# Four products without a reader after each step of TensorE while the first image is set up

## What is computed

```python
def block0(x):                       # attention, 8 heads of 16 channels, L = 1024 pixels
    hid = group_norm(x, 32 groups)
    q, k, v = qkv_w @ hid + qkv_b
    weight = softmax((q * scale).T @ (k * scale))     # 1024 x 1024 for each head and image
    a = weight @ v
    return x + proj_w @ a + proj_b

def block1(x):                       # 1x1 convolution and a feed-forward network of 512 features
    x = x + conv_w @ gelu(rmsnorm(x)) + conv_b
    return x + ffn_w2 @ gelu(ffn_w1 @ rmsnorm(x) + ffn_b1) + ffn_b2
```

## Time and profile before

| | |
|---|---|
| median of 3 runs | 1762.37 us (1761.8 to 1763.55) |
| time of the profiled execution | 1763.75 us |
| its span, first to last instruction | 1761.8 us |
| mean granted clock over the span | 0.975 |
| PE busy | 1698.3 us, 96% |
| DVE busy | 1492.8 us, 85% |
| ACT busy | 1366.5 us, 78% |
| POOL busy | 335.7 us, 19% |
| DMA | 106.18 MB, mean 60 GB/s |

### The profile page before, as it was taken

One profiled execution on the slowest core, in us unless ns is written; L12 is line 12 of the kernel. 1 busy time (PEld: TensorE's weight loads), 2 busy tenths in 40 slices (PEclk: granted clock), 3 DMA queues, 4 the chain that ended last, 5 costly groups with the idle time before them and its releaser, 6 DMA issues.

```text
span 1761.8 us, 33312 instructions
## 1 busy us (share of the span) xinstructions
PE 1698.3 (96%) x12402; PEld 693.2 (39%) x12402; DVE 1492.8 (85%) x2606; ACT 1366.5 (78%) x2480; POOL 335.7 (19%) x411
## 2 busy tenths in 40 slices
PE   3999999999999999999999999999999997699999
PEld 2333333333333333333333333333333332355555
DVE  4899999999999999999999999999999992455552
ACT  1288888888888888888888888888888887466664
POOL 4101111111111111111111111111111011322220
PEclk8599999999999999999999999999999999799999
DMA  5422323232323132324242324141313011233341
GB/s 111 64 44 52 61 41 71 46 66 43 70 40 73 40 72 38 76 37 75 36 76 37 76 36 76 33 67 35 67 35 66 10 21 38 79 104 110 107 109 72
DMA packets 61121, 106.18 MB, mean 60 GB/s; under 512 B 27296, under 2 KB 30112, under 8 KB 60960
## 3 DMA queue, kind: packets, MB, share of 16 engines
q1 hardware_dynamic: 58656, 95.66, 27.6%
q10 hardware_dynamic: 2304, 8.39, 1.2%
HBM read 34.48 MB, written 9.06 MB: 25 GB/s over the span
## 4 chain that ended last, share of the span: by engine, by line
PE 83%; DVE 11%; issue 2%; SPq 1%; DMA 1%; POOL 1%; ACT 1%; DVEq 0%; ACTq 0%; POOLq 0%
PE psum L607 26%; PE psum L578 25%; PE psum L591 10%; DVE maxes L865 9%; PE psum L673 6%; PE psum L561 4%; PE psum L645 2%; PE psum L647 2%; PE psum L646 2%; PE psum L549 2%; PE psum L514 2%; PE psum L690 1%; DVE stats L881 1%; DVE rows L849 1%; SPq L309 0%
## 5 line engine op out<-in xcount | busy, mean ns | idle before, releaser
L865 DVE TENSOR_REDUCE maxes<-psum 128x1 f32<-128x512 f32 x2048 | 1269.5, 680 | 92.3 <-PE psum L578 90.8
L779 ACT ACTIVATE probs<-psum 128x512 f32<-128x512 f32 x2048 | 1107.4, 600 | 219.2 <-PE psum L591 196.6
L578 PE MATMUL psum<-k_stack,q_stack 62*128 62x512 f32 x2048 | 785.6, 461 | 19.0 <-DVE maxes L865 8.9
L591 PE MATMUL psum<-q_stack,k_stack 64*128 64x512 f32 x2048 | 770.8, 455 | 1.2 <-ACT probs L779 1.1
L607 PE MATMUL psum<-probs,values 128*32 128x256 f32 (+1 forms) x6912 | 621.2, 431 | 0.5 <-ACT probs L779 0.5
L578 PEld LDWEIGHTS psum<-k_stack,q_stack 62*128 62x128 f32 x2048 | 329.5, 188 | 561.8 <-DVE maxes L865 445.7
L591 PEld LDWEIGHTS psum<-q_stack,k_stack 64*128 64x128 f32 x2048 | 318.7, 185 | 14.8 <-ACT probs L779 10.5
L607 PEld LDWEIGHTS psum<-probs,values 128*32 128x32 f32 x6912 | 136.2, 108 | 286.8 <-issue 228.7
L673 PE MATMUL psum<-probs,inv_den 128*128 128x512 f32 x256 | 116.5, 598 | 0.0
L411 POOL CAST parts<-neg_max 128x16 fp32r<-128x16 f32 x64 | 12.6, 196 | 538.2 <-DVE neg_max L841 538.2
L788 ACT ACTIVATE probs<-psum,params_sb 128x512 f32<-128x512 f32 x128 | 82.5, 685 | 20.6 <-PE psum L647 14.2
(11 more groups left out here) (82 smaller groups left out, 1044.6 us busy)
## 6 DMA issues: line engine op xcount, KB each, us to landing
q_stack<-q_high SPq DMA_DIRECT2D x256, 64.0 KB, 2.2
k_stack<-k_high SPq DMA_DIRECT2D x128, 128.0 KB, 4.0
x_sb<-in_x SPq DMA_DIRECT2D x16, 512.0 KB, 5.2
q_stack<-q_low SPq DMA_DIRECT2D x128, 64.0 KB, 4.0
k_stack<-k_low SPq DMA_DIRECT2D x64, 128.0 KB, 4.3
attn<-raw SPq DMA_DIRECT2D x128, 64.0 KB, 2.3
inv_den<-inv_den_rows SPq DMA_DIRECT2D x128, 64.0 KB, 2.3
values<-inv_rms_rows SPq DMA_DIRECT2D x16, 512.0 KB, 5.0
```

Of the source, the lines that this page charges most:

```text
L578: nc.tensor.matmul(psum[:, BANKS + tile % BANKS, :], q_stack[used, place, chunk // 4, p, 128 * (chunk % 4):128 * (chunk % 4) + 128], k_sta ...
L591: nc.tensor.matmul(psum[:, tile % BANKS, :], k_stack[used, place, p, 128 * chunk:128 * chunk + 128], q_stack[used, place, t, p, :], start= ...
L779: nc.scalar.activation(probs[:, tile % 8, :], psum[:, tile % BANKS, :], ACT.Exp, scale=SCALE).then_inc(probs_ready, 1)
L865: nc.vector.tensor_reduce(maxes[:, chunk // 4, j, 4 * p + chunk % 4, key_half:key_half + 1], psum[:, BANKS + max_tile(u, s, k) % BANKS, :] ...
```

## The change

In TensorE's stream a new function `keep_awake(n)` issues `n` products of the projection weights (`wp`, 128 by 128) with the matrix of the group means (`group_mean`, 128 by 128) into the first 128 columns of `acc`. They wait for nothing and signal nothing, and nobody reads what they write: the first real product into `acc` starts a new sum. Four of them follow each of the steps 10 to 15 of u = -2, and each step of u = -1 that is not broken.

That makes 6 x 4 = 24 products in u = -2. In u = -1, steps 0 to 2 have 12, all ahead of the first maximum tile, and steps 4, 5, 7, 8, 9, 11, 12, 14 and 15 have 36, each group of four between the last maximum tile of one step and the first of the next. 72 products are added in all, and nothing is taken away or moved.

```diff
+            def keep_awake(n):
+
+                for i in range(n):
+                    nc.tensor.matmul(acc[:, 0:C], wp[:, :], group_mean[:, :], start=True, stop=True)
+
             def slot(b, parity, half, part=None):
                 u = b * 2 + half
                 for s in steps_of(part):
...
                     weigh_before(u, parity, half, s, 0 if broken else QUARTER, HALF)
+                    if u == -1 and not broken or u == -2 and s >= 10:
+                        keep_awake(4)
```

## The result

The median went from 1762.32 us (4 runs, 1761.8 to 1763.55) to 1774.79 us (4 runs, 1772.72 to 1776.99). The ratio is 1.007, with a 95% interval of 1.0052 to 1.0087. The forecast was 1757.1, and the range ended at 1763.0. The profiled execution took 1776.99 us with a span of 1775.0, 13.2 more than the span before.

The account below looks back on a forecast made before the run. A chain paced by VectorE, with TensorE at half clock last at four broken steps, was taken as the bound. 5.8 + 0.3 + 2.25 - 1.2 - 1.9 = 5.25 us won, from 1762.37 to 1757.1; range 1754.2 to 1763.

Parts of the forecast that it names:

- What bounds the start: Up to unit 0: VectorE's reductions set the pace at about 0.605 us each, TensorE only at four broken steps.
- the check of the model: Broken steps at half clock: a modelled VectorE wait of 1.6 us, set against 1.44 to 1.82 in the trace.
- The gap: Before the first maximum tile: 0.2 us for the products and 1.7 for 3.4 us at half clock; tile 1.9 later.
- case B: The forecast: the clock falls in the gap and comes back in the fill; 1757.1 us, chance 0.44.
- The price per product: In the gap at full clock: 0.22 to 0.27 us per product, 8.5 us taken for the 36.
- The groups: Nine groups of four between maximum tiles: 0.13 us of VectorE waiting each at full clock, 1.2 us lost in all.
- The four breaks: Side jobs in the four broken steps: VectorE waits 0.4 us in place of 6.18 at full clock, 5.8 won.
- The first steps of unit 0: First tile of unit 0 to the group mean of step 3: 2.25 us won from the full clock.
- The ends of case B: Whole kernel: 1755.5 to 1759.5 us, given as following from the ends of the terms.
- Case C: Nine groups among the maxima at half clock cost 1.6 us each; slower, 1773 or 1785 us, chance 0.16.
- Case A: In the gap the clock never falls, so the 1.7 us are not lost; 1755.4 us, chance 0.28.
- The 5.3 us in the earlier trace: End of the attention: the clock came back after 5.3 us of dense products, called float32, in one place.

Follow-up runs that it names:

- e10: e9 plus one product at the end of each of the four broken steps; 1756.8 us, ratio 0.9967 to the kernel before.
- e1: The change with only its 36 products in the gap before the first maximum tile, without the nine groups between tiles; 1763.1 us, ratio 0.9999 to the kernel before.
- e5: The change with eight early products at steps 7 and 8 of u = -2, four fewer at step 2, and the nine groups moved to mid-step; 1760.8 us.
- e7: The change with eight early products at steps 7 and 8 of u = -2, four fewer at step 2 of u = -1, nine groups at step ends; 1772.7 us.
- e11: e7 with groups of four at the ends of all 13 steps from step 3 of u = -1, broken ones included; 1759.1 us, ratio 0.9984 to the kernel before.
- e9: e5 with each group of four split into three products behind the second tile and one behind the fourth; 1764.7 us, ratio 1.0009 to the kernel before.
- e3: The change with one product after each maximum tile, except at side jobs, in place of the nine groups; 1800.2 us, ratio 1.020 to the kernel before.
- e8: Early gap products as in e7, but using 64 rows instead of 128, and no groups between maximum tiles; 1762.5 us, one run.

## Why the prediction was wrong

**What bounds the start: right.** VectorE's rate between the breaks, its waits at half clock, and the way of the gain to the end all came out. (The fourth break waits 1.10 in the earlier trace rows, less than the 1.44 to 1.82 that the check of the model named.) In e10, where the clock is full, the group mean is at 79.85; the forecast for it was 80.8.

**The gap: the mechanism right, the size too small.** The clock fell and came back in the fill, as in case B, but it was down for about seven microseconds and not 3.4. The first tile came 3.2 late instead of 1.9. The price per product was right: at full clock e1 made the 36 in 8.28 us, where the sum had 8.5.

**The groups: this is the step that failed.** The sum put nine of them at 0.13 us each, 1.2 in all, on a clock that case B held full for the whole of the maxima. They cost 14.6, or 1.6 each, and 1.6 is what the prediction itself gave for a group at half clock. I took it that the mix of tiles and products as a whole would hold the clock, and did not look at the order in it. The order was in the code: a break in mid-step, then two tiles, then a whole step of tiles, and only then a group. e5 shows that the places count: the same nine groups in mid-step made the kernel 11.8 us faster than e7. e11 shows that more groups need not cost more: with four more, and behind the breaks, it was 13.5 us faster than e7. The price at full clock was a little low, 0.13 against 0.2 to 0.3 in e11; nine times that would be 1 us more and not 13. That the stretch of tiles alone is what makes the clock fall is an argument from these medians, and it is not shown: the falls in the traces of e7 and e11, and e9 against e5, do not fit it.

**The four breaks:** 6.18 to 0.4 was the sum; it was 3.8, with 0.20 at the one that ran wholly at full clock; in e10 the four wait 0.20, 0.29, 0.28 and nothing. **The first steps of unit 0:** 2.25 was the sum, 1.7 came, the clock being back at 96 only. **The ends of case B:** 1755.5 to 1759.5 are not what the ends of its terms add up to; by them it is 1753.8 to 1762.1, and 1774.8 is outside these too.

**The rivals.** Case C had the place, the mechanism and nearly the time: "if the clock falls once the maxima have begun", 1773. That the time came so near is in part luck: its sum had eight groups and 12.8 us where 14.6 came, 0.2 for the gap where the first tile came 3.2 late, and left out the 1.7 won in unit 0; these errors partly cancel. It had 0.16, and with a mechanism that the before trace showed for 39 us at a stretch, that was too little. The error was one of weight: the only rows on tiles with products among them were those around 83, where the clock rose, and those have both kinds of scores. For the order of the change there was no row at all, and the range should have held both ends of that: it stopped at 1763 where 1773 was worked out. Case A was seen in the gap of e1, and it is worth little by itself. The 5.3 us in the earlier trace rows were misread besides: the prediction calls them float32 products, but they are products of the type fp32r with all 128 rows, one record each (and not float32, as the text ahead of it says of all matmuls but the scores):

```profile
1521.69 0.77 PE L645 MATMUL psum<-q_stack,wconv_high 128*128 128x512 f32 x1 [1.08 <-ACT attn L757]
...
1526.94 0.47 PE L645 MATMUL psum<-q_stack,q_high 128*128 128x512 f32 x1
```

In the Trainium skill, "TensorE: Matmul & The Clock Gate", section "What's actually happening", the clock follows how busy the engine was. Busy time as the profile counts it does not show that here: from 68 to 76 TensorE is busy for 7.64 of 8 us at 0.50 in the changed kernel and for 7.49 at 1.00 in e10. (From 60 to 75 in the kernel before it was not quite without a break, as the prediction has it, but paused twice for 0.36 us. And the stacks of image 1 are wanted 19 steps of 2.8 us, some 53 us, behind the start of unit 0, and not 44. Nothing hangs on either.)

**What stays open.** Why the clock fell in some executions of e5, e9 and e11 and not in others, at 38.7 in e7, and at 53 in e3 without any change in the pattern, is not settled; no run moved only the moment at which a pattern begins. Nor is it settled what tells the tiles of maxima from the products: e8 speaks against the number of rows in the gap. The type fp32r alone is not it either, since the clock came back at 1527 behind 5.3 us of such products in the kernel before. Type, rows and the waits between tiles were not tried apart among the tiles. Each kernel has one trace, so when and where the clock fell is known for one execution of each.

## What to carry to other kernels

Filler work for the clock is a bet on the clock: where it stands between the steps of another engine's chain, it cost 0.2 to 0.3 us here per group at full clock, and 1.8 of its 2.1 at half. So work out both prices, look for the longest stretch that is left without it, above all behind the places where the regular pattern is broken: to fill these made falls of the clock rarer here (e9 to e10), for reasons that stay open. Judge such a version by the spread of many runs, since one execution with a full clock says little about the next.

## What the runs showed that I had not expected

At full clock one product alone between two score tiles holds TensorE for 0.42 us, four in a row for 1.09 (e3 and the earlier trace rows); so fillers come cheaper in threes and fours than singly. The clock stayed full over 2.28 us of idle time in one execution and fell within 1.58 in another (e1 and the change). In e11 it fell at 43.6 with no idle time above 0.69 us in the seven microseconds before. And products of 64 rows held it in the gap as well as products of 128 (e8, one execution).
